# Building the slot tables of a routed expert stage from four chunks of 16 steps instead of 64 single steps

## What is computed

```
def _L0_ffn_ref(x, router_w, w1, w2, w3):
    B, T, C = x.shape
    flat = x.reshape(-1, C)
    logits = flat @ router_w.T
    probs = jax.nn.softmax(logits, axis=-1)
    topk_probs, topk_idx = jax.lax.top_k(probs, TOP_K)
    topk_probs = topk_probs / (jnp.sum(topk_probs, axis=-1, keepdims=True) + 1e-09)
    onehot = jax.nn.one_hot(topk_idx, N_EXPERTS, dtype=flat.dtype)
    gates = jnp.einsum('nk,nke->ne', topk_probs, onehot)
    h1 = jnp.einsum('nc,ehc->neh', flat, w1)
    h3 = jnp.einsum('nc,ehc->neh', flat, w3)
    h = jax.nn.silu(h1) * h3
    y = jnp.einsum('neh,ech->nec', h, w2)
    out = jnp.einsum('ne,nec->nc', gates, y)
...
    x = x + _L0_conv_ref(_ln_c(x), ...)
    t = _to_tokens(x)
    t = t + _L0_ffn_ref(_ln_t(t), L0_ffn_router_w, L0_ffn_w1, L0_ffn_w2, L0_ffn_w3)
```

## Time and profile before

| | us |
|---|---|
| median of 3 runs | 1087.97 |
| lowest and highest of them | 1083.72, 1092.55 |
| the profiled execution, its own time | 1088.35 |
| its span | 1086.4 |
| TensorE busy | 855.5 |
| VectorE busy | 722.1 |
| ScalarE busy | 624.2 |
| GpSimd busy | 302.3 |

### The profile page before, as it was taken

One profiled execution on the slowest core, in us unless ns is written; L12 is line 12 of the kernel. 1 busy time (PEld: TensorE's weight loads), 2 busy tenths in 40 slices (PEclk: granted clock), 3 DMA queues, 4 the chain that ended last, 5 costly groups with the idle time before them and its releaser, 6 DMA issues. The chain is left out here.

```text
span 1086.4 us, 21188 instructions
## 1 busy us (share of the span) xinstructions
PE 855.5 (79%) x6788; PEld 578.2 (53%) x6788; DVE 722.1 (66%) x1924; ACT 624.2 (57%) x1285; POOL 302.3 (28%) x337
## 2 busy tenths in 40 slices
PE   4992257999999618498888848996768999958497
PEld 2771226999999608366666634443443444425232
DVE  7896796654444266688888866887685444445775
ACT  4661104554444245688888836885756777746353
POOL 3156007777777522300000010112130001025100
PEclk9895557999999856599999977998897999989699
DMA  4001713310100120111111000000100000000000
GB/s 131 2 1 38 115 34 88 100 38 21 26 23 19 32 73 1 40 50 40 58 39 58 30 20 1 1 1 28 33 1 1 1 0 0 0 19 5 1 1 39
DMA packets 25272, 32.70 MB, mean 30 GB/s; under 512 B 11582, under 2 KB 14665, under 8 KB 24814
## 3 DMA queue, kind: packets, MB, share of 16 engines
q1 hardware_dynamic: 20206, 27.50, 8.9%
q0 software_dynamic: 4992, 4.22, 1.6%
HBM read 19.31 MB, written 4.91 MB: 22 GB/s over the span
## 5 line engine op out<-in xcount | busy, mean ns | idle before, releaser
L1822 DVE SCALAR_TENSOR_TENSOR routed_hid_stage<-ps,routed_act_stage 128x512 f32<-128x512 f32 (+1 forms) x117 | 70.5, 603 | 103.7 <-ACT routed_act_stage L1590 101.9
L1590 ACT ACTIVATE routed_act_stage<-ps 128x512 f32<-128x512 f32 x117 | 69.9, 597 | 88.8 <-PE ps L1895 88.8
L1905 PE MATMUL ps<-w_sb,routed_hid_stage 128*128 x936 | 118.2, 270 | 0.0
L1895 PE MATMUL ps<-routed_x_stage,w_sb 128*128 128x256 f16 x858 | 116.0, 278 | 2.4 <-ACT routed_x_stage L1598 2.4
L1152 ACT ACTIVATE hid_stage<-ps,b_col_sb 128x512 f32<-128x512 f32 x192 | 116.1, 695 | 0.4 <-PE ps L1103 0.3
L1905 PEld LDWEIGHTS ps<-w_sb,routed_hid_stage 128*128 128x128 f32 x936 | 114.6, 193 | 1.5
L412 POOL TENSOR_TENSOR st_sb<-st_sb,neg_half_sb 128x4 f32 (+1 forms) x32 | 37.5, 1172 | 251.7 <-DVE st_sb L407 251.7
L1646 POOL DMA_INDIRECT routed_got_stage<-expert_rows,take_stage x78 | 81.8, 1049 | 78.2 <-DVE give_stage L1797 54.7
L1103 PE MATMUL ps<-x_sb,w_sb 128*128 (+1 forms) x384 | 97.9, 401 | 1.8 <-ACT hid_stage L1152 1.8
L1117 PE MATMUL ps<-hid_stage,w_sb 128*64 128x512 f32 x384 | 94.4, 610 | 1.3 <-DVE gated_stage L1184 1.3
L1895 PEld LDWEIGHTS ps<-routed_x_stage,w_sb 128*128 x858 | 84.8, 104 | 11.2 <-issue 2.8
(11 more groups left out here) (403 smaller groups left out, 1817.5 us busy)
## 6 DMA issues: line engine op xcount, KB each, us to landing
w_stage_sb<-f_w SPq DMA_DIRECT2D x32, 176.0 KB
x_sb<-w_sb SPq DMA_DIRECT2D x16, 256.0 KB, 2.4
rt_sb<-vals_stage SPq DMA_DIRECT2D x16, 256.0 KB, 2.3
rel_bias_sb<-bias_bands SPq DMA_DIRECT2D x16, 128.0 KB
w_stage_sb<-f_w SPq DMA_DIRECT2D x14, 128.0 KB, 2.8
w_sb<-f_w SPq DMA_DIRECT2D x1, 1536.0 KB
routed_got_stage<-expert_rows,take_stage POOLq DMA_INDIRECT x78, 2.5
expert_out<-routed_rows_stage,give_stage POOLq DMA_INDIRECT x78
```

The lines of the kernel that those rows point to most:

```text
L1590: nc.scalar.activation(act_h[:, n, :], ps[:, H1 + (q + n) % 2, :], ACT.Silu, scale=UNSCALE).then_inc(h_act, 1)
L1822: last = nc.vector.scalar_tensor_tensor(hid[:, q % 2, n, 0:full], ps[:, H3 + (q + n) % 2, 0:full], UNSCALE, act_h[:, n, 0:full], ALU.mult, ...
L1895: last = nc.tensor.matmul(o, w16[:, part, bass.ds(col, P)], xb[:, q % 2, :], start=(part == 0), stop=(part == 1))
L1905: last = nc.tensor.matmul(ps[:, Y + q % 2, h * C:(h + 1) * C], hid[:, q % 2, n, a * BLK + h * P:a * BLK + (h + 1) * P], w2[:, bass.ds(e * ...
```

## The change

The 64 steps are grouped into four chunks of 16 (`PER_CHUNK`). For a chunk, VectorE writes three half-precision arrays in one instruction each: the column one-hots of 16 steps (78 x 16 elements per partition), the row one-hots (128 x 16), and the column one-hots times step number plus one (`turn16`). ScalarE writes a fourth, the column one-hots times the partition number. Step m of the chunk is the innermost index, so that the arrays stand in memory with the 16 steps side by side. TensorE then makes 16 products per chunk, each of 156 columns in place of 78: the two sums (partition, step + 1) come out side by side and need no code. Both operands of such a product are read with a step of 16 elements (32 bytes). Buffers are two deep.

The decode falls from 17 operations plus the copy and two finishing ones to seven. `owner` is made after `give` in place of before. The table `iota16` grows from 128 to 2048 elements per partition on ScalarE. The arrays lie in memory of `sq`, `act_h` and `hid`, which nobody else uses at that time. TensorE gets 54 further products that nobody reads (`spare`, 128 x 512 half precision into PSUM bank 7): 24 before the first chunk, 2 between chunks, 24 after the last. Five load semaphores are merged, with the same waits.

```
+            LIST_CHUNKS = 4
+            PER_CHUNK = TOPK * NT // LIST_CHUNKS
+            iota16 = sbl("sort_iota16", [P, P, PER_CHUNK], F16)
...
-            LOW, SHIFTED, COUNTED, PLACED, OWNED, LISTED = 0, 3, 4, 5, 6, 7
+            LOW, SHIFTED, COUNTED, PLACED, LISTED, OWNED = 0, 3, 4, 5, 6, 7
...
-                    nc.scalar.copy(iota16[:, :], iota)
-                    nc.scalar.activation(row_code[:, :], pcol, ACT.Copy, scale=1.0 / 1024, bias=1.0).then_inc(s_prepared, 1)
+                    nc.scalar.copy(iota16[:, :, :], iota.unsqueeze(2).broadcast_to((P, P, PER_CHUNK)))
+                    nc.scalar.activation(turn16[:, :], iota[:, 0:TOPK * NT], ACT.Copy, bias=1.0).then_inc(s_prepared, 1)
...
                     nc.scalar.activation(rt[:, 1, :, :], rt[:, 1, :, :], ACT.Exp).then_inc(s_prepared, 1)
+                    for n in range(LIST_CHUNKS):
+                        act.wait_ge(s_hot, n + 1)
+                        nc.scalar.activation(coded[:, n % 2, 0, :, :], hot_col[:, n % 2, :, :], ACT.Copy,
+                                             scale=pcol).then_inc(coded_row, 1)
...
-                    nc.vector.scalar_tensor_tensor(row, col, -float(P), slot, ALU.mult, ALU.add).then_inc(s_routing, 1)
+                    nc.vector.tensor_copy(col16[:, :].rearrange("p (k t) -> p k t", k=TOPK), col)
+                    nc.vector.scalar_tensor_tensor(row16[:, :].rearrange("p (k t) -> p k t", k=TOPK), col, -float(P), slot,
+                                                   ALU.mult, ALU.add).then_inc(s_routing, 1)
...
-                    for n in range(TOPK * NT):
-                        if n >= 4:
-                            dve.wait_ge(s_products, FOUND + n - 3)
-                        k, t = n // NT, n % NT
-                        code = (1.0 + n % 4 / 4) * 2.0 ** (n // 4)
-                        nc.vector.tensor_scalar(hot_slot[:, n % 4, :], iota16[:, :], row[:, k, t:t + 1], code,
-                                                ALU.is_equal, ALU.mult)
-                        nc.vector.tensor_scalar(hot_col[:, n % 4, :], iota16[:, 0:COLS0], col[:, k, t:t + 1],
-                                                row_code[:, 0:1], ALU.is_equal, ALU.mult).then_inc(s_hot, 1)
...
+                    def of_chunk(v, n, rows):
+                        return v[:, n * PER_CHUNK:(n + 1) * PER_CHUNK].unsqueeze(1).broadcast_to((P, rows, PER_CHUNK))
+
+                    for n in range(LIST_CHUNKS):
+                        if n >= 2:
+                            dve.wait_ge(s_products, FOUND + n - 1)
+                        nc.vector.tensor_tensor(hot_col[:, n % 2, :, :], iota16[:, 0:COLS0, :], of_chunk(col16, n, COLS0),
+                                                ALU.is_equal).then_inc(s_hot, 1)
+                        nc.vector.tensor_tensor(hot_slot[:, n % 2, :, :], iota16[:, :, :], of_chunk(row16, n, P),
+                                                ALU.is_equal)
+                        dve.wait_ge(s_hot, n + 1)
+                        nc.vector.tensor_tensor(coded[:, n % 2, 1, :, :], hot_col[:, n % 2, :, :], of_chunk(turn16, n, COLS0),
+                                                ALU.mult).then_inc(coded_turn, 1)
+
+                    dve.wait_ge(s_products, FOUND + LIST_CHUNKS)
+                    n1, flat, second, free = (found[:, n, :] for n in range(4))
+                    c.link(nc.vector.tensor_scalar(n1, ps[:, LIST, COLS0:2 * COLS0], -1.0, None, ALU.add))
+                    c.link(nc.vector.scalar_tensor_tensor(flat, ps[:, LIST, 0:COLS0], float(NT), n1, ALU.mult, ALU.add))
...
-                    for n in range(TOPK * NT):
-                        pe.wait_ge(s_hot, n + 1)
-                        nc.tensor.matmul(ps[:, LIST, 0:COLS0], hot_slot[:, n % 4, :], hot_col[:, n % 4, :],
-                                         start=(n == 0), stop=(n == TOPK * NT - 1)).then_inc(s_products, 1)
-                    pe.wait_ge(s_routing, LISTED)
+                    def spare(n):
+                        for _ in range(n):
+                            nc.tensor.matmul(ps[:, SPARE, :], idn16[:, :], x16[:, 0:GTOK], start=True, stop=True)
+
+                    spare(24)
+                    for n in range(LIST_CHUNKS):
+                        if n:
+                            spare(2)
+                        pe.wait_ge(coded_row, n + 1)
+                        pe.wait_ge(coded_turn, n + 1)
+                        for m in range(PER_CHUNK):
+                            last = nc.tensor.matmul(ps[:, LIST, 0:2 * COLS0], hot_slot[:, n % 2, :, m],
+                                                    coded[:, n % 2, :, :, m].rearrange("p w c -> p (w c)"),
+                                                    start=(n + m == 0), stop=(n * PER_CHUNK + m == TOPK * NT - 1))
+                        last.then_inc(s_products, 1)
+                    spare(24)
+                    pe.wait_ge(s_routing, OWNED)
```

More of the change, by code:

```diff
@@ L1547, in _ @@
                 def _(sp):
-                    load(sp, "sort", consts[:, :], sort_d)
+                    load(sp, "const", consts[:, :], sort_d)
                     for n in range(CHUNKS_FIRST):
@@ L1745, in _ @@
                     c.link(nc.vector.tensor_tensor(rest, ranked, base.unsqueeze(1).broadcast_to((P, NT, E)), ALU.add))
-                    slot, raw, col, row = (pos[:, n, :, :] for n in range(4))
+                    slot, raw, col = (pos[:, n, :, :] for n in range(3))
                     for k, hot in enumerate((hot1, hot2)):
@@ L1768, in _ @@
-                    c.link(nc.vector.tensor_tensor(ends[:, :, :], iota[0:1, 0:NB].unsqueeze(2).broadcast_to((1, NB, E - 1)),
-                                                   last_[0:1, 0:E - 1].unsqueeze(1).broadcast_to((1, NB, E - 1)), ALU.is_ge))
-                    c.link(nc.vector.tensor_reduce(owner_f[:, :], ends[:, :, :], AX.X, ALU.add))
-                    nc.vector.tensor_copy(owner[:, :], owner_f[:, :]).then_inc(s_routing, 1)
-                    dve.wait_ge(s_products, FOUND + TOPK * NT)
@@ L1774, in _ @@
-                    n1, flat, second, free, quarter, part = (found[:, n, :] for n in range(6))
-                    power, fraction = found_bits[:, 0, :], found_bits[:, 1, :]
-                    c.link(nc.vector.tensor_copy(flat, ps[:, LIST, 0:COLS0]))
-                    bits = flat.bitcast(mybir.dt.int32)
-                    c.link(nc.vector.tensor_scalar(fraction, bits, 0x7FFFFF, 0x3F800000, ALU.bitwise_and, ALU.bitwise_or))
-                    c.link(nc.vector.tensor_scalar(power, bits, 23, None, ALU.logical_shift_right))
@@ L1780, in _ @@
-                    fraction = fraction.bitcast(F32)
-                    c.link(nc.vector.tensor_scalar(quarter, fraction, 4.0, -4.45, ALU.mult, ALU.add))
-                    c.link(nc.vector.tensor_scalar(quarter, quarter, 12582912.0, None, ALU.add))
-                    c.link(nc.vector.tensor_scalar(quarter, quarter, 12582912.0, None, ALU.subtract))
-                    c.link(nc.vector.tensor_scalar(part, quarter, 0.25, 1.0, ALU.mult, ALU.add))
-                    c.link(nc.vector.reciprocal(part, part))
@@ L1792, in _ @@
-                    c.link(nc.vector.scalar_tensor_tensor(flat, part, float(NT), n1, ALU.mult, ALU.add))
+                    def of_chunk(v, n, rows):
[10 more added lines that the diff above has]
+                                                ALU.mult).then_inc(coded_turn, 1)
@@ L1798, in _ @@
                                                    ALU.mult, ALU.add).then_inc(s_routing, 1)
+                    c.link(nc.vector.tensor_tensor(ends[:, :, :], iota[0:1, 0:NB].unsqueeze(2).broadcast_to((1, NB, E - 1)),
+                                                   last_[0:1, 0:E - 1].unsqueeze(1).broadcast_to((1, NB, E - 1)), ALU.is_ge))
+                    c.link(nc.vector.tensor_reduce(owner_f[:, :], ends[:, :, :], AX.X, ALU.add))
+                    nc.vector.tensor_copy(owner[:, :], owner_f[:, :]).then_inc(s_routing, 1)
                     dve.wait_ge(s_prepared, EXPED)
@@ L2406, in _ @@
                 def _(sp):
-                    load(sp, "l2", map_w[:, :], L2)
+                    load(sp, "maps", map_w[:, :], L2)
                     load_small(sp, F2)
@@ L2656, in _ @@
                 def _(sp):
-                    load(sp, "l3", cw[:, :, :], L3)
+                    load(sp, "maps", cw[:, :, :], L3)
                     load_small(sp, F3)
```

40 lines of the change are left out of this document (19 added, 21 removed).

## The result

The changed kernel takes 1080.63 us (median of 11 runs, 1076.9 to 1083.28) against 1085.75 for the one before (11 runs). The ratio is 0.9947, with a 95% interval of 0.9926 to 0.9967: 5.8 us faster, 3.6 to 8.0. The forecast was 15.3. One of the eleven runs before, at 1573 us, counts in the median and not in the ratio. The profiled execution took 1081.72 us, its span 1079.9.

A forecast was written before the change was run, and what follows sets the result against it. One chain, from VectorE's 64 steps through `owner`, decode and first gather to the first transpose, was taken to bound the start. Terms moved the gather from 165.03 to 149.7, 15.3 us: 1088.35 to 1073.0 us, range 1067 to 1083.

The forecast's parts named there:

- the price of one product on TensorE: List chunks on TensorE: 0.137 us per 156-column product, bounds 0.07 and 0.32; only the last chunk's 2.2 us on the path.
- The prediction's own sign of being wrong: List chunks: the prediction is wrong if VectorE waits for TensorE between chunks.
- TensorE becomes the bound through the strided reads: Rival, list chunks: 0.27 us a product, 4.4 a chunk, list done 9.1 us later, 1082 us; chance 0.11.
- spares between the chunks at 0.45 us a pair: TensorE between chunks: two spare products, 0.45 us, make a chunk 2.65 us, just what VectorE needs.
- that the clock, once up, stays up: TensorE behind the list: 24 trailing spares at 0.24 us, 5.7 us in all, end at 152.6, ahead of the first transpose.
- VectorE's operations: Chunk arrays on VectorE: three half-precision operations at 0.81, 1.23 and 0.81 us, a chunk 2.6 us, four 10.4.
- the first rival: Chunk arrays: VectorE stays at one element a cycle, 4.97 us a chunk, 9.5 us later, 1082.5 us; chance 0.11.
- the first chunk was ready: Start of the list: first chunk ready at 136.6, leading spares end at 136.8, so they cost nothing.
- The decode from its first operation to `give`: Behind the list: seven operations, 1.55 us to the start of `give`, in place of 5.14 us for decode and `owner`.
- the expert stage moves as a whole: Expert stage: GpSimd's queue starts with the first gather, so the stage moves by what that gather moves, 15.3 us.
- The cover for a late TensorE: Expert stage: TensorE alone starting earlier or later gains or loses nothing, up to some 3.8 us.
- a warm start: First expert blocks: up to 2.5 us faster on TensorE if spares leave the clock up; counted as nothing.

The follow-up runs named there:

- the probe: Changed kernel plus eleven groups of 12 unread 156-column products after the trailing spares, steps given as (weights, moving operand); 1101.81 us, one run.
- the second profile of before: The kernel before, run again unchanged for one more profile; 1085.59 us, a single run.
- pairs of steps: Changed kernel with chunk arrays laid out 8 x rows x 2, so TensorE reads with a step of 2 elements, spares kept; 1069.74 us, ratio 0.9814.
- the steps outermost: Changed kernel with the 16 steps outermost, so TensorE's operands are contiguous and VectorE's token operand repeats one element; 1079.75 us, ratio 0.9931.

## Why the prediction was right or wrong

**Wrong: the price of one product on TensorE.** The prediction wrote "I take 0.137 (full clock with a penalty of two, or the low clock with none)", between 0.07 and 0.32. It was 0.288. It had no row for a strided read and went by the nearest contiguous ones, a nearness of shape and not of access. The row that carried the upper bound, 2.06 ns a column, was nearer the truth (0.288 / 156 = 1.85 ns) than those that it chose, by luck: it is a full-precision product and no strided one. Worked on, a chunk's products are 4.61 us, not 2.2. They exceed VectorE's 2.6, so all four are on the path and not the last alone, and so are the three pairs of spares. Four times 4.61 and three times 0.83 are 20.9 us behind the leading spares. The list ended 60.2 us after the constants' load instead of 146.9 - 97.47 = 49.4. Those 10.8 us are the whole miss: 15.3 - 10.8 = 4.5, and the first gather came 4.3 earlier. The prediction's own sign of being wrong is in the trace: VectorE waits for TensorE between chunks, 2.41 and 2.77 us.

**The rival that came true** was "TensorE becomes the bound through the strided reads", with 1082 us at 0.27 us a product. Measured were 1080.6. It ascribed the 0.27 to the low clock and a penalty of two together; the probe shows that the clock has no part in it. That its price was so near is luck in part, as is its time: it had the spare pairs warm, 1.4 us for 2.5, and its list done 1.7 us too early (156.0, measured on the same scale 157.7). Its chance of 0.11 looks too low: what spoke for it was a mechanism of this very kernel (every element that a product reads lies 32 bytes from the last), and no row spoke against it.
The Trainium skill (SBUF — State Buffer, section "Door 1: The DMA port swizzle") has the 16-byte line and a penalty for each new one; the probe agrees for the moving operand, with 1.8 ns a line. It also says that two hits in a line are enough for full bandwidth. At the full clock that doesn't hold here: a step of 4 elements, two in a line, cost 0.141 us against 0.067. For the weights' reads no such price showed: nothing in the probe's (16,1) against (1,1), 0.006 us a product in the list.

**Wrong in a small part: spares between the chunks at 0.45 us a pair.** They took 0.83 (by the earlier trace rows two cold products of 512 columns are 0.89; the 2.65 us for a chunk had 0.45 for the pair, which is one cold product). The sum had them free; on a full TensorE they cost 2.5 us, as the run without spares shows (2.4).

**Wrong: that the clock, once up, stays up,** on which the 0.24 us for a trailing spare rested. It reached 0.95 in the first chunk and was 0.50 in the next three, without a pause of TensorE. That cost nothing in the products and made the spares cold. The trailing 24 took until 165.6, 7.1 us, and ended just ahead of the first transpose (0.16 us idle), so the term "cost nothing" held.

**Right:** VectorE's operations, 0.81, 1.22 and 0.80 us against 0.81, 1.23 and 0.81; so the first rival, VectorE at the single rate, fell. It took the repeat of a single element to bring it about (2.28 us for 2048).
The Trainium skill (VectorE: DVE Perf Modes, section "The perf-mode tier table") has the twofold rate for such operands; the trace agrees, 1.22 us for 2048 elements.
**Also right:** the first chunk was ready at 137.37 and the leading spares ended at 137.52. This profile runs 0.75 later than before's (98.22 against 97.47), so these are 136.6 and 136.8 as forecast. The decode from its first operation to `give`: 1.58 us against 1.55. `give` to gather 1.21 and 4.3 to the first transpose, unchanged. `owner` behind `give` and the larger table cost nothing that shows: VectorE's first chunk operation starts 36.5 us after the constants' load (134.71), before 36.3 (133.76), and the difference is the cast's 0.2. Decode and owner together are 4.0 of the 4.3 us gained.

**Right: the expert stage moves as a whole** with the first gather. It is 208.3 us against 208.8 of the second profile of before. The cover for a late TensorE, put at 3.8 us at most, is some 2.5 us by the probe; in the changed kernel nothing came near it, since the trailing spares ended in time. That a warm start was counted at nothing was right too, by the two stages without spares (207.8 and 207.7 us).

**Right: the mechanism of the forecast,** once the products are cheap. With pairs of steps VectorE sets the pace, the gather comes at 51.1 against the 52.2 forecast, and the time is 1069.7 against 1073.0. Of the 1.1 us of the gather 1.0 is the last chunk's products at the full clock, 1.17 us against 2.2. The other 2 us of the time are within the spread of the runs.

## What to carry to other kernels

When one engine writes a layout so that it can work at twice the rate, price the other engine's reads of it in that layout, by the bytes between the elements and not by the count of columns. A layout with two half-precision elements side by side served both engines here: VectorE kept its rate, TensorE its own, and it beat the version before and the changed one (1069.7 us against 1085.8 and 1080.6, and by the ratios to before 0.978 to 0.985 against 0.993 to 0.997). Spare work that keeps a clock up is free only where the engine waits; between chunks on a full TensorE it cost its own length.

## What the runs showed of the hardware

- A moving operand costs 1.8 ns for each new 16 bytes that it enters, at clock 1.00 and at 0.50 alike (0.282 and 0.283 us for 156 columns at a step of 16 and of 8). Half of it at a step of 4 (0.141). Weights read at a step of 16 cost nothing in the probe (0.067 us a product either way) and some 0.006 us a product in the list (0.079 against 0.073).
- The clock fell under moving reads at a step of 16. It was 1.00 ahead of the strided chunks and of the probe's strided groups, and fell to 0.50 in both, with TensorE busy 4.61 of 4.61 us. Without spares it never rose in 18.5 us of such products without a pause. At a step of 4 it stayed 1.00, with TensorE busy 10.40 of 10.40 us, and with pairs too, with waits of 0.81 us in each chunk. It fell under contiguous products as well: with the steps outermost and waits of 1.85 to 3.26 us between the chunks it was 0.50 from 145 to 158 us. Why is not shown by these runs.
- VectorE with an innermost repeat of a single element fell to the single rate (2.28 us for 2048), with a pair kept double rate (1.22), and with pairs that it reads 32 bytes apart came out between (2.01).
